# Token stage of a vision tower on one core: three pixel buffers instead of two, eight groups written out, no ninth group's statistics

## The reference

```python
B, C, H, Wd = img.shape                                  # 64, 3, 224, 224
h, w = (H // P, Wd // P)                                 # 14, 14 patches of 16 x 16
x = img.reshape(B, C, h, P, w, P)
x = jnp.transpose(x, (0, 2, 4, 3, 5, 1)).reshape(B, h * w, P * P * C)
x = _layernorm(x, ln1_g, ln1_b)                          # over 768 values of a patch
x = jnp.einsum('bnp,pd->bnd', x, W_proj) + b_proj        # 768 -> 192
x = _layernorm(x, ln2_g, ln2_b)
cls = jnp.broadcast_to(cls_token, (B, 1, cls_token.shape[-1]))
x = jnp.concatenate([cls, x], axis=1)
x = x + pos_embedding
```

## Time and profile before

| | us |
|---|---|
| median of 3 runs | 5335.71 |
| lowest, highest | 5334.87, 5339.04 |
| profiled execution, its own time | 5334.58 |
| span of that execution (first to last instruction) | 5332.9 |

### The profile page before, as it was taken

One profiled execution on the slowest core, in us unless ns is written; L12 is line 12 of the kernel. 1 busy time (PEld: TensorE's weight loads), 2 busy tenths in 40 slices (PEclk: granted clock), 3 DMA queues, 4 the chain that ended last, 5 costly groups with the idle time before them and its releaser, 6 DMA issues. The chain is left out here.

```text
span 5332.9 us, 93616 instructions
## 1 busy us (share of the span) xinstructions
PE 4815.6 (90%) x31272; PEld 4488.6 (84%) x31272; DVE 3383.1 (63%) x9581; ACT 2280.7 (43%) x6373; POOL 561.8 (11%) x529
## 2 busy tenths in 40 slices
PE   4775899899899989989998998998999699999999
PEld 4774699799889979978987997997899699999999
DVE  4555566566756756665674675667567466666666
ACT  2443555465365445536545544553654122222221
POOL 1122000000000000000000000000000233333332
PEclk8887899899899989989999998998999799999999
DMA  6452000000000000000000000000000100000000
GB/s 135 103 123 48 10 1 1 20 1 1 11 10 1 1 20 1 1 20 1 1 1 20 1 1 20 1 1 17 3 1 1 41 18 17 16 15 18 18 18 18
DMA packets 66789, 101.13 MB, mean 19 GB/s; under 512 B 3774, under 2 KB 62269, under 8 KB 62715
## 3 DMA queue, kind: packets, MB, share of 16 engines
q1 hardware_dynamic: 62907, 91.53, 6.8%
q0 software_dynamic: 944, 2.42, 0.3%
q10 hardware_dynamic: 2560, 2.36, 0.2%
HBM read 67.10 MB, written 29.20 MB: 18 GB/s over the span
## 5 line engine op out<-in xcount | busy, mean ns | idle before, releaser
L600 ACT ACTIVATE att_prob<-att_s,att_npeak 99x198 f32<-99x198 f32 x1536 | 640.7, 423 | 1131.0 <-DVE att_npeak L741 1128.1
L741 DVE TENSOR_REDUCE att_npeak<-att_s 99x2 f32<-99x396 f32 x768 | 435.7, 567 | 806.8 <-PE att_s L891 803.1
L917 PE MATMUL att_o<-att_probT,att_vx 99*96 99x198 f32 (+1 forms) x3072 | 672.0, 341 | 10.6 <-ACT att_probT L610 10.6
L891 PE MATMUL att_s<-att_kx,att_qx 96*99 96x198 f32 (+1 forms) x3072 | 645.0, 332 | 7.6 <-ACT att_vx L586 7.6
L1265 PE MATMUL ffn_y<-ffn_down,ffn_hidden 128*128 128x192 f32 x3564 | 635.8, 329 | 7.1 <-DVE ffn_acc L1176 5.2
L1265 PEld LDWEIGHTS ffn_y<-ffn_down,ffn_hidden 128*128 128x128 f32 x3564 | 588.4, 191 | 29.7 <-DVE ffn_acc L1176 27.7
L917 PEld LDWEIGHTS att_o<-att_probT,att_vx 99*96 99x96 f32 (+1 forms) x3072 | 496.3, 179 | 58.2 <-issue 32.1
L891 PEld LDWEIGHTS att_s<-att_kx,att_qx 96*99 96x99 f32 (+1 forms) x3072 | 507.0, 165 | 22.9 <-issue 11.1
L1046 POOL TENSOR_TENSOR ffn_hidden<-ffn_relu 128x384 f32<-128x384 f32 x462 | 379.3, 827 | 764.3 <-ACT ffn_relu L1073 457.1
L758 DVE TENSOR_SCALAR att_prob<-att_prob,att_total 99x198 f32<-99x198 f32 x1536 | 427.8, 322 | 26.9
L902 PEld LDWEIGHTS att_t<-att_ident,att_prob 99*99 99x99 f32 x3072 | 383.9, 166 | 55.9 <-DVE att_prob L758 52.4
(11 more groups left out here) (209 smaller groups left out, 9813.5 us busy)
## 6 DMA issues: line engine op xcount, KB each, us to landing
tok_pixels<-in_x SPq DMA_DIRECT2D x24, 1568.0 KB
att_hid<-hidden SPq DMA_DIRECT2D x9, 1188.0 KB
ffn_hid<-hidden SPq DMA_DIRECT2D x34, 288.0 KB, 2.9
hidden<-att_resid SPq DMA_DIRECT2D x8, 1188.0 KB
out_hidden<-ffn_acc SPq DMA_DIRECT2D x33, 288.0 KB, 2.3
hidden<-tok_rows SPq DMA_DIRECT2D x8, 1176.0 KB
att_oT<-in_L_attn_qkv_w ACTq DMA_DIRECT2D x1, 1536.0 KB, 11.1
tok_posb<-in_L_tok_pos_embedding POOLq DMA_DIRECT2D x1, 1176.0 KB, 42.7
```

The costliest lines, as they stand in the source:

```text
L600: ins = nc.scalar.activation(prob[:, i % 2, h, :], s_bank[i % 2][0:HALF, h * NTOK:(h + 1) * NTOK], ACT.Exp, bias=npeak[:, i % 2, h:h + 1], ...
L741: nc.vector.tensor_reduce(npeak[:, i % 2, :], s_bank[i % 2][0:HALF, 0:2 * NTOK].rearrange("p (h k) -> p h k", h=2), AX.X, ALU.max, negate= ...
L891: ins = nc.tensor.matmul(s_bank[i % 2][0:HALF, h * NTOK:(h + 1) * NTOK], qx[0:K, p % 2, head, q0:q0 + HALF], kx[0:K, p % 2, head, b * NTOK ...
L917: ins = nc.tensor.matmul(o_bank[j % 2][0:M, 0:NTOK], vx[:, p % 2, 2 * b + k, v0:v0 + M], probT[:, j % 2, k * NTOK:(k + 1) * NTOK], start=( ...
```

## The change

Three pixel buffers (`SLOTS` = 3) with a semaphore each: loads 0, 1 and 2 are issued at the start, and load g + 3 goes out when group g has been normalised. The four-pass loops of SP, ACT and DVE become eight groups written out (POOL's and PE's loops stay). In group 7 the wait for pixels, the statistics of a ninth group, their 14 aggregations, ScalarE's square root, the reciprocal and the shift are left out, and so is SP's semaphore increment. DVE's wait for `rows_out` is left out for groups 0 and 1.

```diff
+    SLOTS = 3
-        pixels = m.sb("pixels", [P, 2, CH, XROW])
+        pixels = m.sb("pixels", [P, SLOTS, CH, XROW])
...
-        pixels_in = [m.sem(f"pixels_in{s}") for s in range(2)]
+        pixels_in = [m.sem(f"pixels_in{s}") for s in range(SLOTS)]
...
-                load(0, 0)
-                load(1, 1)
-                with sp.Fori(0, (GROUPS - 2) // 2) as pair:
-                    gg = pair * 2
-                    for s in range(2):
-                        sp.wait_ge(normed_made, (gg + s + 1) * SIDE)
-                        load(gg + s + 2, s)
-                        store(gg + s, s)
-
-                sp.sem_inc(pixels_in[0], 16 * CH)
-                for s in range(2):
-                    store(GROUPS - 2 + s, s)
+                for g in range(SLOTS):
+                    load(g)
+                for g in range(GROUPS):
+                    if g + SLOTS < GROUPS:
+                        sp.wait_ge(normed_made, (g + 1) * SIDE)
+                        load(g + SLOTS)
+                    store(g, g % 2)
...
-                with act.Fori(0, GROUPS // 2) as pair:
-                    gg = pair * 2
-                    for s in range(2):
-                        g = gg + s
+                for g in range(GROUPS):
+                    s = g % SLOTS
...
-                        deviation1(g + 2)
+                    if g + 1 < GROUPS:
+                        deviation1(g + 2)
...
-                with dve.Fori(0, GROUPS // 2) as pair:
-                    gg = pair * 2
-                    for s in range(2):
-                        g = gg + s
-                        st = Steps(dve, dve_step, 2 + g * PER_GROUP)
-                        dve.wait_ge(pixels_in[1 - s], gg * (8 * CH) + 16 * CH * (s + 1))
+                for g in range(GROUPS):
+                    s, more = g % 2, g + 1 < GROUPS
+                    st = Steps(dve, dve_step, 2 + g * PER_GROUP)
+                    if more:
+                        dve.wait_ge(pixels_in[(g + 1) % SLOTS], 16 * CH * ((g + 1) // SLOTS + 1))
...
-                            if wv < SIDE:
-                                ins = statistics1(1 - s, wv)
+                        if wv < SIDE and more:
+                            ins = statistics1((g + 1) % SLOTS, wv)
...
+                    if more:
                         dve.wait_ge(normed_made, (g + 1) * SIDE)
                         aggregate(st, mv1, stat1, mv1_made)
-                        aggregate(st, mv2, stat2, mv2_made)
+                    aggregate(st, mv2, stat2, mv2_made)
+                    if more:
                         scale_shift1(st, g + 2)
```

More of the change, by code:

```diff
@@ L132, in _, with load @@
                     sp.sem_inc(s, PRIMED)
-                def load(g, s):
+                def load(g):
                     for c in range(CH):
-                        sp.dma_start(pixels[:, s, c, :], x_rows[c, :, bass.ds(g * GB, GB), :]).then_inc(pixels_in[s], 16)
+                        sp.dma_start(pixels[:, g % SLOTS, c, :], x_rows[c, :, g * GB:(g + 1) * GB, :]
+                                     ).then_inc(pixels_in[g % SLOTS], 16)
                 def store(g, s):
                     sp.wait_ge(rows_made, g + 1)
-                    sp.dma_start(hid_rows[:, bass.ds(g * GB, GB), :], rows[:, s, :, :]).then_inc(rows_out[s], 16)
-                load(0, 0)
-                load(1, 1)
-                with sp.Fori(0, (GROUPS - 2) // 2) as pair:
-                    gg = pair * 2
-                    for s in range(2):
-                        sp.wait_ge(normed_made, (gg + s + 1) * SIDE)
-                        load(gg + s + 2, s)
-                        store(gg + s, s)
-                sp.sem_inc(pixels_in[0], 16 * CH)
-                for s in range(2):
-                    store(GROUPS - 2 + s, s)
+                    sp.dma_start(hid_rows[:, g * GB:(g + 1) * GB, :], rows[:, s, :, :]).then_inc(rows_out[s], 16)
+                for g in range(SLOTS):
[5 more added lines that the diff above has]
+                    store(g, g % 2)
                 for s in range(2):
@@ L172, in _ @@
                 deviation1(1)
-                with act.Fori(0, GROUPS // 2) as pair:
-                    gg = pair * 2
-                    for s in range(2):
-                        g = gg + s
[L177 to L188, removed]
+                for g in range(GROUPS):
+                    s = g % SLOTS
+                    act.wait_ge(shift1_made, g + 1)
+                    normalise(s, 0, g * SIDE)
+                    for wv in range(SIDE):
+                        v, t = wv % 2, g * SIDE + wv
+                        if wv + 1 < SIDE:
+                            normalise(s, wv + 1, t + 1)
+                        act.wait_ge(turned, t + 1 + PRIMED)
+                        for i in range(2):
+                            ins = nc.scalar.activation(patchT[:, v, 3 * i:3 * i + 3, :],
+                                                       t_bank[v][i][:, 0:3 * P].rearrange("p (k n) -> p k n", k=3),
+                                                       ACT.Copy)
+                        ins.then_inc(patchT_made, 1)
+                    if g + 1 < GROUPS:
                         deviation1(g + 2)
-                        act.wait_ge(mv2_made, g + 1)
-                        nc.scalar.activation(rstd2[:, :, :], mv2[:, :, 1:2], ACT.Sqrt, bias=eps[0:P, :]).then_inc(sd2_made, 1)
+                    act.wait_ge(mv2_made, g + 1)
+                    nc.scalar.activation(rstd2[:, :, :], mv2[:, :, 1:2], ACT.Sqrt, bias=eps[0:P, :]).then_inc(sd2_made, 1)
             @block.gpsimd
@@ new lines, in _ @@
+                for g in range(GROUPS):
[3 more added lines that the diff above has]
+                        dve.wait_ge(pixels_in[(g + 1) % SLOTS], 16 * CH * ((g + 1) // SLOTS + 1))
+                    dve.wait_ge(rows_normed, g + PRIMED)
+                    for wv in range(SIDE + 1):
+                        t = g * SIDE + wv - 1
+                        if wv:
+                            dve.wait_ge(projected, t + 1)
+                            nc.vector.tensor_tensor(y[:, wv - 1, :], y_bank[(wv - 1) % 2][0:P, 0:DIM], bias[:, :], ALU.add
+                                                    ).then_inc(y_made, 1)
+                        if wv < SIDE and more:
+                            ins = statistics1((g + 1) % SLOTS, wv)
+                            if wv == SIDE - 1:
+                                st.did(ins)
+                        if wv:
+                            dve.wait_ge(y_made, t + 1 + PRIMED)
+                            st.did(nc.vector.bn_stats(stat2[:, wv - 1, :], y[:, wv - 1, :]))
+                    if more:
@@ L288, in _ @@
                         dve.wait_ge(normed_made, (g + 1) * SIDE)
                         aggregate(st, mv1, stat1, mv1_made)
-                        aggregate(st, mv2, stat2, mv2_made)
+                    aggregate(st, mv2, stat2, mv2_made)
+                    if more:
                         scale_shift1(st, g + 2)
-                        dve.wait_ge(sd2_made, g + 1)
-                        st.did(nc.vector.reciprocal(rstd2[:, :, :], rstd2[:, :, :]))
-                        st.settle()
@@ L295, in _ @@
[L295 to L301, removed]
+                    dve.wait_ge(sd2_made, g + 1)
@@ new lines, in _ @@
+                    st.did(nc.vector.reciprocal(rstd2[:, :, :], rstd2[:, :, :]))
+                    st.settle()
+                    if g >= 2:
+                        dve.wait_ge(rows_out[s], 16 * (g // 2) + PRIMED)
+                    for wv in range(SIDE):
+                        ins = nc.vector.tensor_scalar(rows[:, s, wv, :], y[:, wv, :], mv2[:, wv, 0:1], rstd2[:, wv, :],
+                                                      ALU.subtract, ALU.mult)
+                        if wv == SIDE - 1:
+                            ins.then_inc(rows_normed, 1)
@@ L303, in _ @@
+                    assert st.n == (PER_GROUP if more else PER_GROUP - 2), st.n
             @block.tensor
```

## The result

The kernel after the change takes **5371.4 us** (median of 4, 5360.07 to 5376.4) against 5335.29 us (4 runs, 5333.92 to 5339.04). The ratio is 1.0066, 95% interval 1.0052 to 1.0081: 36 us slower, where 68 us of gain were forecast. The profiled execution took 5376.4 us, its span is 5374.7 us.

What follows compares the result with a forecast made beforehand. Token-stage stalls on DVE's pixel waits, a transfer latency and no lack of bandwidth, were taken as the bound. 67.6 - 0.35 + 0.9 = 68.2 us off the median of 5335.71 gave 5267.5 us, range 5261 to 5277.

Steps and rivals of the forecast that it cites:

- The bound and the six waits: Token stage, groups 1 to 6: DVE's pixel waits, 12.8 us each, set the pace and all six go.
- rival A: Opening loads: load 1 is held up by load 2, everything comes 27 us later, gain 41, 5294 us; chance 0.03.
- The period's size: Token stage: a group's period falls from 54.27 us to 43.0, between 42.65 and 43.33; six periods give 67.6 us.
- No ninth group: Group 7: without the 14 extra aggregations, ScalarE's second square root takes the first one's place, gaining 0.9 us.
- GpSimd and transfers beside DVE: Token stage: POOL's passes (11.8 us) and the transfers now run beside DVE's work and the steps, each at cost 0.
- D: Token stage: DVE is held while GpSimd works, 11.8 us replacing the 12.8 us wait, 5329 us; chance 0.02.
- E: Token stage: transfers beside each other take over 42.65 us per group; at 45 us, gain 55, 5281 us; chance 0.02.
- B: Token stage: PE's lower clock lasts longer after each restart, 0.7 to 1 us more per group, 5273 to 5275; chance 0.07.
- C: Token stage: PE's clock stays low through a group's steps, 2.53 us more per step, up to 5515 us; chance 0.01.
- Written-out groups: Token stage: writing the loops out costs 0, with a range up to three fetch waits of 2.5 us (7.5 us).
- a shift of the later stages: Stages behind the token stage change in length; with several fetch stalls it was the rest, chance 0.02.
- the prediction's own sign of being wrong: Wrong if the token stage's period stays above 44 us or later stages change by more than the runs' spread.

Runs made afterwards that it cites:

- e4: The kernel before the change with 95 semaphore increments added on DVE at the end of the token stage: 5431.0 us.
- e6: The changed kernel with 33 semaphore increments added on DVE at the end of attention instead of the token stage: 5315.9 us.
- e2: The changed kernel with 28 semaphore increments added on ScalarE at the end of the token stage, none on DVE: 5368.1 us.
- e1: The changed kernel with 33 semaphore increments added on DVE at the end of the token stage: 5268.9 us.
- e3: The changed kernel with 33 semaphore increments added on DVE and 28 on ScalarE at the end of the token stage: 5263.8 us.
- e8: The changed kernel with 115 semaphore increments added on DVE at the end of the token stage: 5316.6 us.
- e9: The changed kernel with 109 semaphore increments added on DVE at the end of the token stage: 5314.6 us.
- e7: The changed kernel with 100 semaphore increments added on DVE at the end of the token stage: 5263.1 us.
- e10: The changed kernel with 16 semaphore increments added on DVE at the end of the token stage: 5265.8 us.

## Why the prediction was wrong

By its steps:

- **The bound and the six waits: right.** The periods of the changed kernel are (357.24 - 101.94) / 6 = 42.55 us, just under the 42.65 to 43.33 forecast, and 54.27 before. Load 3 and its followers were never waited for, and load 1 was not held up (rival A): DVE's first statistics of group 0 came at 65.48 us.
- **The period's size: 0.45 us too long.** I took the middle between group 7's short slow pass and the six long ones. In the changed kernel the first pass behind the gap alternates, short in groups 2, 4 and 6 and near group 1's old length in the others. Groups 2 and 3:

```profile
147.91 2.60 PE L330 MATMUL tok_y<-tok_w,tok_patchT 128*112 128x192 f32 x12
...
189.84 3.80 PE L330 MATMUL tok_y<-tok_w,tok_patchT 128*112 128x192 f32 x12
```

  The periods alternate with it, 42.9 to 43.2 us as forecast and 41.9 to 42.1, which no term of the prediction had. The six periods gave 6 x (54.27 - 42.55) = 70.3 us where 67.6 were forecast, group 0 came 2.1 us earlier, and group 7 took 41.92 us, 0.7 less. 70.3 + 2.1 + 0.7 is the 73.2 measured, to rounding; 68.2 were forecast.
- **No ninth group: right.** Without the first 14 aggregations the row phase of group 7 starts 1.69 us after its aggregations begin (397.47 to 399.16); with them it took 3.01 (354.23 to 357.24 in group 6). The skipped part is 1.3 us against the 0.9 forecast.
- **GpSimd and transfers beside DVE: right**, nothing was held (rivals D and E). GpSimd's passes took 5.84 to 5.93 us beside DVE's work, and the gaps before each group stayed at 4.7 us; PE's granted clock was 0.98 and 0.99 in the steady parts of groups 1 and 2 (106 to 144 and 148 to 186 us), so rivals B and C did not come.
- **Written-out groups: this step failed.** I asked where the longer code costs in the token stage, found nothing, and put 0 to 7.5 us. That was right for the token stage: it has 11 packets on queue 14 instead of 4 and no issue wait on DVE. I did not ask where the code *behind* it goes. The sum has no term for attention and the experts at all: it takes "stages behind it as long as before" without a reason, and what the runs show in its place is 63.4 us more in attention and 51.6 us more in the experts. The row that could have raised the question was on the table: the earlier trace rows showed 2.5 us in each of 7 passes at a loop's head, and I took it as the price of a loop that might vanish, not as a price that every loop behind the change could start to pay. The forecast gave "a shift of the later stages" a share of 2% with "several fetch stalls"; it measured 115 us, and the prediction's own sign of being wrong, later stages that change by more than the spread of the runs (4.2 us), came true.

How the 115 us come about, as far as shown. In the experts, DVE stands 45.2 + 11.6 us at the head in 15 passes, 3.8 us each; PE waits for it (`ffn_r` for DVE's `ffn_x`: 57.9 us in 32 times against 26.5), the pass takes 70.5 us in place of 67.35, and 16 x 3.12 = 50 of the 51.6 us are there. In attention DVE's extra stall is 5.05 us in each of 7 passes, 35 us of 63. In the pass shown, PE stands 15.20 us for the first normalised tile, against 4.37 and then 1.80 and 6.53 before: the first normalisation comes 5.05 us later and now falls beside GpSimd's operation of 6.65 us, so that it takes 6.45 us; before, a later one did. Most passes are 6.9 us longer (457.4 against 450.5), and two of the changed kernel's passes another 7 to 9. e4 has 51.9 us, e6 49.7 and e2 53.1 in attention, so about 50 us belong to the place; the other 10 or so are no more than what e1 and e3 differ by.

Only about half of the loss is time in which PE stands idle. The other half is TensorE's clock. One pass of attention, 2816 matmul records, before, then a usual and a long one after (stretch, its length, what PE, PEld, DVE, ACT and POOL are busy for, granted clock, DMA share, GB/s; the clock is a mean of the two levels, 0.5 for 1.2 GHz and 1 for 2.4 GHz):

```profile
3706.94:4157.40 450.46, 418.21 (x2816) 385.23 (x2816) 291.00 (x785) 228.36 (x691) 6.65 (x1) 0.95 0.02 7
```
```profile
3690.15:4147.58 457.43, 420.42 (x2816) 387.13 (x2816) 290.60 (x785) 227.70 (x691) 6.65 (x1) 0.94 0.02 7
2311.25:2777.49 466.24, 431.02 (x2816) 397.34 (x2816) 290.93 (x785) 227.80 (x691) 6.76 (x1) 0.92 0.02 7
```

A usual pass is 7.0 us longer than the one before: 4.8 us are idle time of PE, 2.2 us the same work at a lower mean clock. In the two long passes the clock takes 10.4 and 12.8 us. Over attention PE is busy 3398.0 us against 3364.5 before, over the experts' passes 1087.1 against 1065.9, together 55 of the 115 us. In e6 only attention is badly placed, in e8 and e9 only the experts, and only that stage has the longer busy time (e6: 3385.7 in attention, 1067.6 in the experts; e8: 3365.0 and 1088.6; e9: 3366.5 and 1085.7). So the lower clock comes with the stalls and is no cause of its own, but for the 14 us that e1 and e3 differ by. Why it falls more in some passes than in others was not traced.

The Trainium skill ("Runtime: NRT & Kernel Launch", Instruction fetch mechanics) has the mechanism: code is fetched ahead in a row, and a taken branch to a page that is not held makes the engine wait for it. The prediction cited it for the loops that go and not for those that stay. The traces agree with the rule, by the packets and stalls that come with it, and not with its sizes on DVE: the page gives blocks of 16 KiB (256 instructions), of which two are held, and here the packets are 8 KB, and a body of 284 instructions either stays or costs five packets a pass. Bad places at 191, 50 and 44 modulo 256 (after, e8, e9), with a good one at 96 (before) between them, don't fit one stretch of 28 in 256.

The kernel that beats both is the change with DVE's later loops placed well: e1, e3, e7 and e10 at 5263 to 5269 us, 1.3% to 1.4% under the kernel before. That the forecast of 5267.5 us lies among them says that the token stage was judged nearly right; it is no merit of the prediction for the kernel as it was changed.

## What to carry to other kernels

When a change alters how many instructions an engine has ahead of a hardware loop, look at every later loop of that engine: a body can begin to be brought in again on every pass when it is moved (here one of 284 instructions), and then the change and its neighbours can't be judged by one run. Compare stage by stage, look for waits put down to issue at the first operations of a loop and for packets on the instruction queue within it, and move the code by some tens of instructions that do nothing before a good change is given up. A pair of buffers whose refill can only start when its reader is done exposes the transfer's latency even where the bandwidth is idle half the time; a third one took all of it away here.

## What was not expected of the hardware

- 33 instructions without any work, placed in idle time, are worth 102 us (5371.4 to 5268.9), 1.9% of this kernel; 95 of them cost the kernel before 94 us.
- Nearly half of what the badly placed code costs is not idle time: TensorE does the same work at a lower mean granted clock, 3398.0 us in place of 3364.5 in attention.
- A badly placed loop brings in more than the one block that doesn't fit: five packets a pass in the experts, where the body touches four blocks by my count. Why four are not held while three are stays open.
- The stall is decided by a few instructions: experts' loop at place 35 pays 0, at 44 it pays 3.0 us a pass, the same as at 50.
